# Router logits with the router as the stationary operand, their turn by VectorE and four transfers, the softmax spread over six units, and the mixing weights turned by VectorE

## The reference

```python
x = x + layernorm(attn(layernorm(x), a_params, B_w, C_w, D))
h = layernorm(x)
router = softmax(h @ w_router)                 # [.., 8]
gate   = softmax((h @ w_gating) / 0.1)         # [.., 8]
cw = router * gate
cw = cw / (sum(cw) + 1e-9)
out = sum over e of cw[e] * ((silu(h @ w_gate[e]) * (h @ w_up[e])) @ w_down[e])   # F = 512
x = x + layernorm(out)
```

## Time and profile before

| | |
|---|---|
| median of 3 executions | 1169.93 us (1169.41 to 1170.9) |
| profiled execution, its own time | 1171.27 us |
| its span, first to last instruction | 1169.4 us |
| TensorE busy | 1144.2 us, 98% of the span |
| VectorE busy | 946.0 us, 81% |
| ScalarE busy | 673.4 us, 58% |
| GpSimd busy | 640.3 us, 55% |
| mean granted TensorE clock | 0.992 of full |

### The profile page before, as it was taken

One profiled execution on the slowest core, in us unless ns is written; L12 is line 12 of the kernel. 1 busy time (PEld: TensorE's weight loads), 2 busy tenths in 40 slices (PEclk: granted clock), 3 DMA queues, 4 the chain that ended last, 5 costly groups with the idle time before them and its releaser, 6 DMA issues.

```text
span 1169.4 us, 16900 instructions
## 1 busy us (share of the span) xinstructions
PE 1144.2 (98%) x5156; PEld 940.8 (80%) x5156; DVE 946.0 (81%) x2045; ACT 673.4 (58%) x1293; POOL 640.3 (55%) x496
## 2 busy tenths in 40 slices
PE   7899999999999999999999999999999999999996
PEld 6678888888888888888888888888888888888885
DVE  8688788888878888787888878878887888878765
ACT  2366565565656556565655656556565655656563
POOL 4467465555646455464555646555454645556453
PEclk8899999999999999999999999999999999999999
DMA  3230210202121020211102121020211102021110
GB/s 122 63 109 28 64 45 16 68 28 73 37 55 37 19 82 28 64 46 37 46 28 73 36 64 46 22 62 28 73 38 48 44 19 82 28 68 33 47 51 12
DMA packets 82696, 57.60 MB, mean 49 GB/s; under 512 B 35344, under 2 KB 64176, under 8 KB 82608
## 3 DMA queue, kind: packets, MB, share of 16 engines
q1 hardware_dynamic: 82608, 56.54, 16.4%
HBM read 48.13 MB, written 8.39 MB: 48 GB/s over the span
## 4 chain that ended last, share of the span: by engine, by line
PE 95%; DVE 3%; issue 1%; POOL 0%; ACT 0%; DMA 0%; POOLq 0%; SPq 0%; ACTq 0%; DVEq 0%
PE g L263 10%; PE u L263 10%; PE u L265 10%; PE u L264 10%; PE g L264 10%; PE g L265 10%; PE y L263 10%; PE y L265 10%; PE y L264 10%; PE n_ps L270 2%; PE m_ps L263 1%; PE m_ps L265 1%; PE m_ps L264 1%; PE m_ps L335 1%; PE y L286 1%; PE m_ps L336 1%
## 5 line engine op out<-in xcount | busy, mean ns | idle before, releaser
L1001 POOL TENSOR_TENSOR hid_lo<-hid,hid_hi 128x512 fp32r<-128x512 f32 x255 | 341.1, 1338 | 410.8 <-ACT hid_hi L493 410.7
L487 ACT ACTIVATE gate<-g 128x512 f32<-128x512 f32 x512 | 306.1, 598 | 340.1 <-PE g L265 339.4
L743 DVE TENSOR_TENSOR hid<-gate,u 128x512 f32<-128x512 f32 x512 | 348.2, 683 | 161.2 <-ACT gate L487 128.6
L493 ACT ACTIVATE hid_hi<-hid 128x512 fp32r<-128x512 f32 x512 | 321.6, 628 | 57.2 <-DVE hid L743 56.5
L263 PE MATMUL g<-xe_hi,w_hi 128*128 128x512 f32 x512 | 206.8, 404 | 0.0
L749 DVE TENSOR_TENSOR hid_lo<-hid,hid_hi 128x512 fp32r<-128x512 f32 x257 | 202.3, 787 | 1.8
L263 PE MATMUL u<-xe_hi,w_hi 128*128 128x512 f32 x512 | 200.2, 391 | 2.3 <-DVE hid L743 2.3
L263 PE MATMUL y<-hid_hi,w_hi 128*128 128x512 f32 x512 | 199.8, 390 | 0.2 <-ACT hid_hi L493 0.2
L265 PE MATMUL g<-xe_hi,w_lo 128*128 128x512 f32 x512 | 199.8, 390 | 0.0
L264 PE MATMUL g<-xe_lo,w_hi 128*128 128x512 f32 x512 | 199.8, 390 | 0.0
L265 PE MATMUL u<-xe_hi,w_lo 128*128 128x512 f32 x512 | 199.7, 390 | 0.0
(11 more groups left out here) (151 smaller groups left out, 1171.1 us busy)
## 6 DMA issues: line engine op xcount, KB each, us to landing
cw_b<-cw_scratch SPq DMA_DIRECT2D x128, 256.0 KB, 3.3
x_sb<-x_in SPq DMA_DIRECT2D x16, 256.0 KB, 3.0
x_out<-o_sb SPq DMA_DIRECT2D x16, 256.0 KB, 2.2
out_scratch<-acc_t SPq DMA_DIRECT2D x60, 64.0 KB, 2.3
ffn<-out_scratch SPq DMA_DIRECT2D x15, 256.0 KB, 2.7
stage<-wgate_in SPq DMA_DIRECT2D x8, 256.0 KB, 2.7
stage<-wup_in SPq DMA_DIRECT2D x8, 256.0 KB, 3.1
stage<-wdown_in SPq DMA_DIRECT2D x8, 256.0 KB, 4.1
```

What stands on the lines that cost most here:

```text
L487: nc.scalar.activation(gate[:, k % 2, :], g_ps[k % 2][:], ACT.Silu).then_inc(gate_ready, 1)
L493: nc.scalar.activation(hid_hi[:, k % RING, :], hid[:, k % RING, :], ACT.Copy).then_inc(hi_ready, 1)
L743: nc.vector.tensor_tensor(hid[:, k % RING, :], gate[:, k % 2, :], u_ps[k % 2][:], ALU.mult).then_inc(hid_ready, 1)
L1001: nc.gpsimd.tensor_tensor(hid_lo[:, k % RING, :], hid[:, k % RING, :], hid_hi[:, k % RING, :].bitcast(f32), ALU.subtract).then_inc(lo_pool, 1)
```

## The change

- The logits of chunks 1 to 15 are made with the router as the stationary operand (32 columns: low and high part by the high xe, high part and zeros by the low xe): two products over 512 tokens. They come out with logits on partitions and tokens along the free dimension. VectorE turns them in 32x32 blocks in unit 27 (`mix_logits_t`), and SyncE moves the four groups of 32 tokens to their partitions with four transfers (`spread_logits`). Chunk 0 keeps the old form (`mix_logits_first`).
- The softmax steps move: VectorE's first part from unit 27 to 30, ScalarE's from 28 to 31, exps from 30 to unit 0 of the next chunk, products from 31 to 1, weights from 1 to 2.
- The mixing weights go into a tile of 128x32, which VectorE turns in 32x32 blocks in unit 3 (`mix_cw_t`); TensorE's transposition and ScalarE's copy go. They are stored with four transfers in place of one.
- The x stage moves: statistics from unit 1 to 3, variance from 2 to 3, GpSimd's root from 2 to 4, normalisation from 3 to 5, TensorE's transposition from behind unit 5 to behind unit 6.
- `keep_warm_split` (24 matmuls of the prologue) goes, and with it its wait.

```diff
-TENSOR_AT = {"turn_cw": 4, "turn_x": 5, "bu": 9, "c": 15, "turn_y": 16, "turn_xe": 26,
+TENSOR_AT = {"turn_x": 6, "bu": 9, "c": 15, "turn_y": 16, "turn_xe": 26,
              "logits": 27}
-SCALAR_AT = {"cw_t": 3, "hi_x": 8, ... "hi_xe": 26, "silus": 28}
+SCALAR_AT = {"hi_x": 8, ... "hi_xe": 26, "silus": 31}
-VECTOR_AT = {"weights": 1, "stats_x": 1, "var_x": 2, "norm_x": 3, ... "softmax": 27, "exps": 30,
-             "products": 31}
-GPSIMD_AT = {"rstd_x": 2, ...}
+VECTOR_AT = {"stats_x": 3, "var_x": 3, "norm_x": 5, ... "logits_t": 27, "softmax": 30,
+             "exps": 0, "products": 1, "weights": 2, "cw_t": 3}
+GPSIMD_AT = {"rstd_x": 4, ...}
...
+            def spread_logits(c):
+                sp.wait_ge(logits_turned, c)
+                sp.wait_ge(raw_read, c)
+                blocks = logits_t[:].rearrange("c (j b q) -> c j b q", j=NT, q=SMALL)
+                for b in range(P // SMALL):
+                    sp.dma_start(raw[b * SMALL:(b + 1) * SMALL].rearrange("p j h q -> p j (h q)"),
+                                 blocks[:, :, b, :]).then_inc(raw_loaded, 16)
...
             def store_cw(c, par):
                 sp.wait_ge(cw_t_ready, c + 1)
-                sp.dma_start(cw_dram[par], cw_t[:]).then_inc(cw_stored, 16)
+                for b in range(P // SMALL):
+                    sp.dma_start(cw_dram[par, :, b * SMALL:(b + 1) * SMALL],
+                                 cw_t[b * SMALL:(b + 1) * SMALL, :]).then_inc(cw_stored, 16)
...
+                if not last:
+                    spread_logits(c + 1)
...
             def mix_turn_x(c):
                 pe.wait_ge(xn_ready, 2 * c + 1)
-                pe.wait_ge(cw_t_ready, c)
...
             def mix_logits(c, par):
                 pe.wait_ge(xe_hi_ready, c + 1)
                 pe.wait_ge(xe_lo_ready, c + 1)
-                for j in range(NT):
-                    t, at = slice(j * P, (j + 1) * P), 4 * E * j
-                    nc.tensor.matmul(m_ps[:, at:at + 4 * E], xe_hi[:, par, t], router[:], start=True, stop=False)
-                    last = nc.tensor.matmul(m_ps[:, at:at + 2 * E], xe_lo[:, par, t], router[:, 0, :], start=False, stop=True)
-                last.then_inc(logits_ready, 1)
+                nc.tensor.matmul(m_ps[0:4 * E, :], router[:, 0:2, :], xe_hi[:, par, :], start=True, stop=False)
+                nc.tensor.matmul(m_ps[0:4 * E, :], router[:, 1:3, :], xe_lo[:, par, :], start=False,
+                                 stop=True).then_inc(logits_ready, 1)
-
-            def mix_turn_cw(c):
-                pe.wait_ge(cw_ready, c + 1)
-                nc.tensor.transpose(n_ps[:, 0:P], cw_pad[:], ident[:]).then_inc(cw_turned, 1)
...
-            pe.wait_ge(act_hi_ready, 1)
-            keep_warm_split()
...
+            def mix_logits_t(c):
+                dve.wait_ge(logits_ready, c + 1)
+                nc.vector.transpose(logits_t[:], m_ps[0:SMALL, :]).then_inc(logits_turned, 1)
...
+                    dve.wait_ge(raw_loaded, RAW_LOADED * c)
...
+            def mix_cw_t(c, first):
+                dve.wait_ge(cw_ready, c + 1)
+                if not first:
+                    dve.wait_ge(cw_stored, CW_STORED * c)
+                nc.vector.transpose(cw_t[:], cw[:]).then_inc(cw_t_ready, 1)
```

More of the change, by code:

```diff
@@ L41 @@
 PIECES = WCOLS // F
-TENSOR_AT = {"turn_cw": 4, "turn_x": 5, "bu": 9, "c": 15, "turn_y": 16, "turn_xe": 26,
+TENSOR_AT = {"turn_x": 6, "bu": 9, "c": 15, "turn_y": 16, "turn_xe": 26,
              "logits": 27}
-SCALAR_AT = {"cw_t": 3, "hi_x": 8, "du": 8, "hi_w": 13, "fin_a": 19, "fin_b": 20, "z_a": 18, "z_b": 18,
-             "hi_xe": 26, "silus": 28}
-VECTOR_AT = {"weights": 1, "stats_x": 1, "var_x": 2, "norm_x": 3, "lo_x": 7, "enter": 8, "scan": 9,
+SCALAR_AT = {"hi_x": 8, "du": 8, "hi_w": 13, "fin_a": 19, "fin_b": 20, "z_a": 18, "z_b": 18,
+             "hi_xe": 26, "silus": 31}
+VECTOR_AT = {"stats_x": 3, "var_x": 3, "norm_x": 5, "lo_x": 7, "enter": 8, "scan": 9,
              "fin_turn": 6, "fin_stats": 14, "fin_var": 14, "fin_shift": 15, "leave": 12, "lo_w": 13, "y": 15, "stats_y": 16, "var_y": 16,
-             "shift": 18, "stats_x1": 22, "var_x1": 22, "norm_x1": 24, "lo_xe": 26, "softmax": 27, "exps": 30,
-             "products": 31}
-GPSIMD_AT = {"rstd_x": 2, "fin_rstd": 15, "fin_add": 21, "rstd_y": 16, "residual": 18, "rstd_x1": 22}
+             "shift": 18, "stats_x1": 22, "var_x1": 22, "norm_x1": 24, "lo_xe": 26, "logits_t": 27, "softmax": 30,
+             "exps": 0, "products": 1, "weights": 2, "cw_t": 3}
+GPSIMD_AT = {"rstd_x": 4, "fin_rstd": 15, "fin_add": 21, "rstd_y": 16, "residual": 18, "rstd_x1": 22}
 LN_EPS = 1e-5
@@ L58 @@
 SMALL = 32
-PROJ = P + D + 2 * E
+PROJ = P + D + 4 * E
+RAW_LOADED = CW_STORED = 16 * (P // SMALL)
 FIN_STORED = 16 * (D // SMALL)
@@ L125, in build @@
         proj_hi, proj_lo = sb("proj_hi", [P, P + D], f32r), sb("proj_lo", [P, P + D], f32r)
-        router = sb("router", [P, 2, 2 * E], f32r)
+        router = sb("router", [P, 3, 2 * E], f32r)
+        logits_t, raw = sb("logits_t", [SMALL, SEQ]), sb("raw", [P, NT, 2, 2 * E])
         a_col, sines = sb("a_col", [NS // 2, 1]), sb("sines", [NS // 2, P])
@@ L136, in build @@
         pr, psum_, den = sb("pr", [P, NT, E]), sb("psum_", [P, NT]), sb("den", [P, NT])
-        cw_pad = sb("cw_pad", [P, P])
-        cw_t = sb("cw_t", [E * NT, P])
+        cw = sb("cw", [P, E * NT])
+        cw_t = sb("cw_t", [P, E * NT])
         stats2, mv2 = sb("stats2", [P, NT, 6]), sb("mv2", [P, NT, 2])
@@ L311, in mix_bu @@
                 else:
-                    pe.wait_ge(raw_read, c)
+                    if c == 1:
+                        pe.wait_ge(raw_read, 1)
+                    else:
+                        pe.wait_ge(logits_turned, c - 1)
                 pe.wait_ge(act_hi_ready, 2 * c + 1)
@@ L328, in mix_turn_xe, with mix_logits_first @@
                 turn(n_ps, lambda j: xn[:, j, :]).then_inc(xe_turned, 1)
+            def mix_logits_first():
+                for j in range(NT):
+                    t, at = slice(j * P, (j + 1) * P), 4 * E * j
+                    nc.tensor.matmul(m_ps[:, at:at + 4 * E], xe_hi[:, 0, t], router[:, 0:2, :], start=True, stop=False)
+                    last = nc.tensor.matmul(m_ps[:, at:at + 2 * E], xe_lo[:, 0, t], router[:, 1, :], start=False, stop=True)
+                last.then_inc(logits_ready, 1)
             def mix_logits(c, par):
@@ L404, in body @@
                     if first and k == 0:
-                        mix_logits(0, 0)
-                    if k == (4 if first else TENSOR_AT["turn_cw"]):
-                        mix_turn_cw(c)
+                        mix_logits_first()
                     if not last:
@@ L527, in body @@
                         mix_silus(0)
-                    if k == (4 if first else SCALAR_AT["cw_t"]):
-                        mix_cw_t(c, first)
                     if not last:
@@ L664, in wide, with mix_softmax_in @@
                 return t.unsqueeze(2).broadcast_to([P, t.shape[1], n])
-            def mix_softmax_in(c):
+            def mix_logits_t(c):
+                dve.wait_ge(logits_ready, c + 1)
+                nc.vector.transpose(logits_t[:], m_ps[0:SMALL, :]).then_inc(logits_turned, 1)
+            def mix_softmax_in(c, first=False):
                 at = SOFT_LINKS * c
                 pair = "p j r -> p (j r)"
[L669 to L673, removed]
+                if first:
+                    dve.wait_ge(logits_ready, 1)
+                else:
+                    dve.wait_ge(raw_loaded, RAW_LOADED * c)
+                src = m_ps[:, 0:NT * 4 * E] if first else raw[:].rearrange("p j h q -> p (j h q)")
+                last = nc.vector.tensor_reduce(out=lg[:].rearrange("p j r e -> p j (r e)"),
+                                               in_=src.rearrange("p (j h q) -> p j q h", j=NT, h=2),
+                                               op=ALU.add, axis=AX.X)
+                last.then_inc(raw_read, 1)
                 dve.wait_ge(raw_read, c + 1)
@@ L891, in body @@
                     if first and k == 0:
-                        mix_softmax_in(0)
+                        mix_softmax_in(0, first=True)
                     if first and k == 1:
@@ L895, in body @@
                         mix_products(0)
-                    if k == (2 if first else VECTOR_AT["weights"]):
+                    if k == VECTOR_AT["exps"] and not first:
+                        mix_exps(c)
+                    if k == VECTOR_AT["products"] and not first:
+                        mix_products(c)
+                    if k == VECTOR_AT["weights"]:
                         mix_weights(c)
+                    if k == VECTOR_AT["cw_t"]:
+                        mix_cw_t(c, first)
                     if k % NB == 0 and k >= 8:
@@ L934, in body @@
                             mix_lo_xe(c + 1, 1 - par)
+                        if k == VECTOR_AT["logits_t"]:
+                            mix_logits_t(c + 1)
                         if k == VECTOR_AT["softmax"]:
```

28 lines of the change are left out of this document (12 added, 16 removed).

## The result

The changed kernel takes 1247.35 us (median of 5, 1246.91 to 1254.22) against 1169.93: ratio 1.0673, 95% interval 1.066 to 1.0686. Slower as forecast, but by 77 us where 33 were forecast, and outside the range.

The account below looks back on a forecast made before the run. TensorE, with no idle time to win back, was taken to bound the kernel. Savings of 7.7 and 1.9, waits of +42.0 and the first chunk's +0.7 made +33.1 us, giving 1203 us; range 1168 to 1230.

Parts of the forecast that it names:

- Savings on TensorE, -9.6: Cheaper logits products save 7.7 us, the mixing weights' transposition leaving TensorE saves 1.9 us.
- The chain and the due time: xn is ready for TensorE's transposition at 9.2 us, due at 8.2: 1.0 us wait per steady chunk without encounters.
- (a): VectorE's queue, with exps and products in units 0 and 1 beside GpSimd, reaches hidden(3) up to 1.4 us late.
- (b): VectorE's variance in unit 3 meets GpSimd's hid_lo(3): up to 1.3 us.
- (c): GpSimd's addition or root in unit 4 meets VectorE's hid_low(4): 0.55 us.
- (d): VectorE's normalisation in unit 5 meets GpSimd's hid_lo(5): 1.06 us.
- the term 42.0 + 1.5: TensorE's waits for xn: 3.0 us per steady chunk, 42.0 in all; the first chunk's from 1.50 to about 3.
- a rival with 12 or 38 us: TensorE's clock falls after waits: 12 us in a third of the chunks, 38 in all; chance 0.12, shared with long waits.
- Other edits: SyncE's logits transfers, VectorE's logits transposition, mixing-weight stores: 0; +1 us per chunk if landing took over twice as long.
- The prologue: Without the 24 warming products TensorE finds the same half clock: 0, up to +2 us if the clock rises later.
- First chunk: Wait before u loses 0.8 of 1.59 us, wait before the transposition rises from 1.50 to about 3: +0.7 us.
- The rival on the other side (no wait): Normalisation is ready when TensorE comes: 1159.5 us; chance 0.15, together with waits under 0.64 us per chunk.

Follow-up runs that it names:

- e1: The changed kernel with the x stage back in its old units: 1178.42 us, ratio 1.0064.
- e7: e1 with the old eight logits products in all chunks, read from PSUM, without transposition or transfers of the logits: 1184.62 us.
- e11: e1 with x statistics in unit 31 of the chunk before, exps behind weigh, normalisation in unit 4 behind hidden(4) and weigh: 1158.83 us, ratio 0.9903.
- e4: The changed kernel with 16 products, whose results are overwritten, ahead of TensorE's wait for xn: 1219.39 us, ratio 1.0417.
- e9: The changed kernel with 8 products, whose results are overwritten, ahead of TensorE's wait for xn: 1231.37 us, ratio 1.0519.
- e5: The changed kernel with TensorE's transposition of xn one unit later, behind unit 7: 1188.72 us, ratio 1.0161.
- e12: e11 with the 24 warming products of the prologue back: 1160.07 us, ratio 0.9913.
- e8: e1 with the x statistics in unit 31 of the chunk before: 1166.89 us, ratio 0.9969.
- e3: The changed kernel with the x stage's root ahead of the addition of expert 7 in GpSimd's unit 4: 1218.53 us, ratio 1.0417.
- e2: The kernel before with only the x stage moved as the change moves it: 1239.88 us, ratio 1.0596.

## Why the prediction was wrong in size

**Savings on TensorE, -9.6: right.** The two logits products start 0.23 apart, and the next matmul 0.23 behind them (e1's rows, shown at e7); e7 gives 0.51 us per chunk in the trace and 6.2 in the medians. e11, with no waits in steady chunks, lies 11.5 us under the kernel before; 9.6 of them were forecast, and its waits at n_ps and u in chunk 0 and 1 are 0.9 shorter. The transposition of the mixing weights (0.12 x 16) wasn't tried alone; a steady chunk takes 69.41 us before and 68.79 in e11, 0.62, where 0.51 + 0.12 were forecast.

**The chain and the due time: right in mechanism, mis-sized.** Where I had 9.2 us without encounters, the trace has (from 729.91) 12.1. The encounters, with their sizes: (a) hidden(3) at 2.36 instead of 1.62, 0.74; (b) the variance operation 0.86 instead of 0.16, 0.70; (c) the root 1.47 instead of 1.02, 0.45; (d) the normalisation 2.05 instead of 1.11, 0.94. They sum to 2.83, and 9.2 + 2.83 is 12.03. I called them races of which one side wins, and took half of 4.3, rounded down (2.0). But the queue is the same in each chunk and so is the outcome: all four were lost, in all 14 steady chunks, with the same sizes within 0.02 us. What each encounter costs is read from the trace; no run takes one away by itself. The waits at n_ps went from 2.1 us (the earlier trace rows and one of 0.6) to 56.5: the term 42.0 + 1.5 measured 54.4.

**The clock: the step that failed.** The sum had 0 for it and left it to a rival with 12 or 38 us, at a chance that it shared with other causes (0.12). e4 measures it at 28.0 us. I reasoned from the earlier trace rows: 1.6 idle, no fall; 2.5 nearly idle, a fall. The wait of 3.0 that I forecast lies beyond both, as the rival itself says, and the sum still had nothing for it: that was the mistake, more than the size of the wait. e9 shows falls with waits of 2.0 us already, in 8 chunks; with 3.8 they come in all, and in 13 of 14 chunks for 6.8 us. Of the 77.4 us, waits and savings make 54.4 - 9.6 = 44.8 and the clock 28.0; most of the 4.6 that are left are the 0.2 behind each wait that e5 shows, 14 x 0.2 = 3, which the sum hadn't either. In the execution with the trace (83 us longer in span) 38 are left beside the 44.8, of them 14 x 2.3 = 33 the clock's in the steady chunks; that execution had the lowest mean clock of the five.

**Other edits.** SyncE's transfers, the logits' transposition (0.70 us), the stores of the mixing weights: 0, right (in the changed kernel VectorE waits for raw once, 0.4 us). The prologue: 0, right; half clock is found either way, and e12 agrees. First chunk: the first wait at u went from 1.59 to 0.83, as said; before the transposition it went from 1.50 to 2.70, where about 3 was said.

**What I gave no price: the softmax in units 0 to 3.** I let it into the sum only as what delays hidden(3). e1 shows that it costs about 1.2 us per chunk (69.97 against 68.79 in e11), once the x stage stands where it stood. This may also be why the x stage was moved: VectorE had no room left there. The room was in unit 31 (e8) and behind hidden(4) (e11).

The rival on the other side (no wait) is out: it needed the addition early, and e3, which takes it off the path to the root, still waits 2.8 us.

## What to carry to other kernels

Where one engine is full and the others run by a hand-written order, walk a moved stage from its first operation to its due time and add what each queue has ahead of it; if the sum misses the due time by a microsecond without any contention, expect the contention too, since here a fixed order lost the same race in every turn. In these runs a wait on TensorE of 2 us or more often cost more than itself: price the half-clock stretch behind it, here about 1.6 us where it was 3.4 us long (e9) and 2.3 where it was 6.8 (the changed kernel against e4). And when a good idea (here: logits at half the price) comes out slower, look for the table entry: the same edits with the x stage and exps placed elsewhere were 1.0% faster than before instead of 6.7% slower.

## What the runs showed of the hardware

An operation of VectorE with two inputs in SBUF, or a normalisation of 128x128 fp32 there, that meets a running two-input operation of GpSimd gets through only once that one has ended, however small it is: 0.86 us instead of 0.16, 1.12 instead of 0.15 (den of 128x4 in e1), 2.05 instead of 1.11. Where VectorE was first, GpSimd's was the longer one (root 1.47 instead of 1.02, hid_lo 1.70 instead of 1.28 in e3). hidden and weigh, which read PSUM, kept their 0.68 beside GpSimd. The Trainium skill (GPSIMD Engine Reference, section Specifications) says that GpSimd's SBUF interfaces are shared with VectorE, with contention against VectorE instructions that have two SBUF inputs; these rows agree.

The clock doesn't follow the length of the idle time alone: in e9 the waits are 2.0 us in all 14 steady chunks, and it falls behind 8 of them. In the profiled executions waits of 1.8 us (e5) brought no fall in 14 chunks, waits of 2.0 (e9) brought 8, waits of 2.8 (e3) 7, of 3.4 to 3.6 (e2) 10, of 3.8 (the changed kernel) all 14. The stretches at half clock behind these waits measured 3.4 or 6.8 us. What decides in which of the chunks it falls stays open, and other executions of the same kernel have other mean clocks (0.952 to 0.962 for the changed one).
